# Vision tower on one core: the next image's first two heads scored in FF2, the head loop two heads ahead

## The chip, the cores and the metric

The kernel runs on one core of one Trainium2 chip. The metric is device time in microseconds of one execution. A core has TensorE (PE, with weight loads as PEld), VectorE (DVE), ScalarE (ACT), GpSimd (POOL) and SyncE (SP, here the issuer of nearly all DMAs), each with its own instruction queue that runs in order and waits on semaphores.

## The reference

Eight images of 256 x 256 go through a wavelet stage, get a class row (257 tokens, width 256), then four transformer layers with 16 heads of 64, and at last a mixture of experts. The part that the change touches is one layer for one image:

```python
q = q.reshape(b, s_len, H, DH); k = ...; val = ...
kr = (r @ W_r[i]).reshape(s_len, H, DH)
AC = jnp.einsum('bqhd,bkhd->bhqk', q + u, k)
BD = jnp.einsum('bqhd,khd->bhqk', q + v, kr)
prob = jax.nn.softmax((AC + BD) * inv_sqrt_d, axis=-1)
vec = jnp.einsum('bhqk,bkhd->bqhd', prob, val).reshape(b, s_len, H * DH)
h = layer_norm(h + vec @ W_o[i], ln1_g[i], ln1_b[i])
ff = jax.nn.relu(h @ W_ff1[i] + b_ff1[i]) @ W_ff2[i] + b_ff2[i]
h = layer_norm(ff, ln2_g[i], ln2_b[i])
```

## The kernel before

Matrices are kept as a high and a low float16 part, and a product is three matmuls (high x high, high x low, low x high: `TERMS`). Nearly every result that PE leaves in a PSUM bank is therefore copied twice: ACT writes the high half, DVE subtracts it from the bank for the low half (`p_part`, `o_part`, `v_part`, the FF1 copies). For queries and keys POOL makes both halves from a float32 copy in `rel`, a ring of four slots.

Each engine has one program, written out by hand: `body(at, l, b, kind)` for each of 32 steps (4 layers of 8 images), image after image. The order of its lines is the order of the queue; there is no planner. Semaphore counts run through (`at(32, n)` is the n-th of 32 signals of this step). Kinds: OPENING (the very first), ENTRY (first image of the layers 1 to 3), MIDDLE (18 of them), CLOSING (last image of the layers 0 to 2), TAIL (layer 3, six images, with expert routing beside it, `kind.routes`) and FINAL.

A step goes through these stages:

- **Class scores** (L1928): the class row of all heads, 24 small matmuls into bank 6; DVE takes the minimum (L2345), ACT the exponential (L2158).
- **Head loop**, h = 0 to 15. PE: scores of head h, four matmuls into the banks 0 and 1 (L1937, L1938), one slot of the next image's projections (`project`, six matmuls, L1844; in the closing step eight projections of positions besides), then `transposes(at, h - 1)` (L1893), four transposes of float32 exponentials into bank 2 or 3. DVE: row minimum of the negated scores with the position term `cb` added, two instructions per head (L2356), key copies (`take_k`, L2258) at odd h, and the low half of head h - 2's transposed exponentials (`p_part`, L2318). ACT: two exponentials per head with the row sum (L2162), query copies at even h (`take_q`, L2097), the high half of head h - 1's transposed exponentials (L2147), and at odd h the class column of two heads (L2187). POOL: both halves of each projection (L1730, L1732) and parts of the norm. The exponentials lie in `E`, a ring of EB = 4 heads.
- **After the loop**: PV products of two heads each (`pv`, L1905, 12 matmuls) for c = 0 and 1, the last head's transposes between them; transposes of the inverse sums and the class columns (L1999); `key` copies; then for c = 0 to 7 a spread of the inverse sums (L2014), the class part (L2018) and the further PV products, with copies on ACT and DVE.
- **W_o** (L2033), the first norm, the next image's values (`project_v`, L1860).
- **FF1**: eight chunks of six matmuls (L2064) into the banks `FB` = 2, 3, 6, 7. For even chunks ACT writes the high half from the bank (L2226), DVE a float32 copy into `rel[:, 0]` (L2474) and the low half from it (L2468). For odd chunks ACT writes float32 into `rel[:, 1]` (L2225) and the high half (L2226), DVE the low half (L2465). `rel[:, 0]` and `rel[:, 1]` are written again only when the previous pair's low half is made (`ff1_lo`).
- **FF2**: 48 matmuls into the banks 4 and 5 (L2076), in the order first output half, chunks 0 to 5; second, chunks 0 to 5; first, 6 and 7; second, 6 and 7. Then ACT's squares (L2236) and DVE's copies (L2504, L2292) for the second norm, whose rest runs inside the next head loop.

SP stacks the projected queries and keys of an image for its scores by DMA (`stack(at, part)`, L1538, 12 DMAs for each half of the heads), after POOL's last split of that half and when the previous image's scores of those heads are done. Before the change the whole loop waits for both halves:

```python
pe.wait_ge(stack_in, at(384, 384))
for h in range(H):
    for qt in range(QT):
        if h:
            pe.wait_ge(s_ok, at(32, 2 * h + qt - 1))
        q = qs[:, h, qt * P:(qt + 1) * P]
```

In the entry steps the class values go to DRAM and come back as `vbd` (`store_vcls`, `load_vbd`) once `class_v` (L1870) has run in the loop at h = 11. Before the first step a prologue projects the first image alone, and ACT loads the position term `cb` by DMA (L2131) between its class values and its first query copy.

## Time and profile before

| | us |
|---|---|
| median of 3 runs (lowest, highest) | 2553.95 (2551.61, 2559.08) |
| the profiled execution: its own time | 2552.9 |
| its span, first to last instruction | 2551.1 |
| PE busy / DVE / ACT / POOL in the span | 2229.0 / 1851.4 / 1599.2 / 1187.2 |
| steps of the image loop, from 174.9 us on | 32 |

The profile shows one execution. A line of the timeline is one instruction (or several merged, xN): start, busy time, engine, line of the kernel, operation, what is written from what, and in brackets the idle time of the engine just before it with what ended it. PE's matmuls are pipelined, so the time from start to start is what one costs the queue, and the busy time of PE is more than that; ACT's and DVE's instructions overlap a little in the same way.

### The profile page before, as it was taken

Reading aid. Unit: us, or ns where it says so; the run is one execution under the profiler, and the core shown is the slowest. Engines: PE = TensorE matmul, PEld = TensorE weight load, DVE = VectorE, ACT = ScalarE, POOL = GpSimd, SP = SyncE. Lnnn points to the kernel's source line nnn. Section 1 sums busy time; section 2 is a strip of 40 time slices with the busy share of each in tenths; the row PEclk is TensorE's granted clock in tenths of the full one; section 3 lists DMA queues with packets and bytes.
Section 4 is the critical chain, followed back from the end, with each engine's and each line's share of the span. In section 5 each row is a group of like instructions: output and inputs, shape, how many; then the busy total and the mean of one; then the engine's idle time right before and its main releaser. Section 6 shows DMA issues by size and latency. Waiting matters only on the chain.

```text
span 2551.1 us, 61172 instructions
## 1 busy us (share of the span) xinstructions
PE 2229.0 (87%) x19318; PEld 1654.4 (65%) x19318; DVE 1851.4 (73%) x5687; ACT 1599.2 (63%) x4853; POOL 1187.2 (47%) x2205
## 2 busy tenths in 40 slices
PE   0249999999989999999989999999899999987998
PEld 0127777777767777777766677777677777665665
DVE  8827777777777777777757777777678877776543
ACT  2216777777667777766656677776677766665322
POOL 3025555554455555554545555554565555541211
PEclk9679999999999999999999999999999999999999
DMA  4354444445554444444644444455533343355110
GB/s 165 83 149 100 123 105 104 110 106 149 148 147 122 108 106 107 108 121 139 183 124 116 111 106 108 102 149 147 151 102 92 98 102 94 98 148 183 51 47 22
DMA packets 378059, 295.35 MB, mean 116 GB/s; under 512 B 45087, under 2 KB 350721, under 8 KB 376739
## 3 DMA queue, kind: packets, MB, share of 16 engines
q1 hardware_dynamic: 370603, 272.41, 41.0%
q10 hardware_dynamic: 4864, 12.68, 1.4%
q0 software_dynamic: 2272, 6.35, 0.7%
q8 instruction: 158, 2.59, 0.4%
q14 instruction: 162, 1.33, 0.2%
HBM read 137.71 MB, written 72.07 MB: 82 GB/s over the span
## 4 chain that ended last, share of the span: by engine, by line
ACT 30%; PE 27%; DVE 15%; issue 7%; SPq 6%; POOL 5%; DMA 4%; DVEq 0%; ACTq 0%; POOLq 0%
ACT e_rows L2162 12%; ACT pt L2147 4%; SPq L1538 4%; PE bk L1279 4%; PE bk L2033 3%; PE bk L2076 3%; PE bk L1905 3%; ACT rel L2097 3%; DVE x L2419 3%; DVE o_rows L2327 3%; ACT pt L2226 2%; PE bk L1893 2%; PE bk L1844 2%; POOL arena L1732 2%; DVE pt L2465 1%
## 5 line engine op out<-in xcount | busy, mean ns | idle before, releaser
L2162 ACT ACTIVATE e_rows<-e_rows,nb 128x257 f32<-128x257 f32 x1024 | 516.8, 516 | 45.8 <-DVE nb L2356 45.1
L2356 DVE CUSTOM_DVE_ANT_0 e_rows<-bk,arena 128x257 f32<-128x257 f32 x1024 | 390.4, 418 | 77.1 <-PE bk L1938 75.8
L1844 PE MATMUL bk<-hin,arena 128*128 128x257 f16 x3072 | 423.5, 275 | 14.3 <-ACT rel L2097 6.9
L2318 DVE TENSOR_TENSOR pt<-bk,pt 128x512 f16<-128x512 f32 x512 | 353.9, 691 | 64.2 <-ACT pt L2147 51.7
L1893 PE MATMUL bk<-ident,e_rows 128*128 128x128 f32 x2048 | 324.1, 281 | 49.3 <-ACT e_rows L2162 28.3
L1732 POOL TENSOR_TENSOR arena<-rel,arena 128x257 f16<-128x257 f32 x496 | 327.3, 660 | 41.3
L1730 POOL TENSOR_SCALAR arena<-rel 128x257 f16<-128x257 f32 x496 | 202.8, 409 | 300.0 <-ACT rel L2097 295.7
L1844 PEld LDWEIGHTS bk<-hin,arena 128*128 128x128 f16 x3072 | 297.8, 98 | 65.1 <-issue 12.9
L2147 ACT ACTIVATE pt<-bk 128x512 f16<-128x512 f32 x512 | 310.1, 606 | 7.0 <-PE bk L1893 7.0
L1893 PEld LDWEIGHTS bk<-ident,e_rows 128*128 128x128 f32 x2048 | 221.6, 141 | 135.1 <-ACT e_rows L2162 113.3
L1937 PE MATMUL bk<-arena 128*128 128x257 f16 x1024 | 256.3, 275 | 12.2 <-DMA arena<-arena 11.7
L1780 POOL TENSOR_SCALAR wf<-wf 128x256 f32<-128x256 f32 x216 | 93.0, 430 | 370.7 <-DMA wf<-in_w_dram 189.7
L1938 PE MATMUL bk<-arena 128*128 128x257 f16 x1024 | 255.9, 275 | 0.0
L1905 PE MATMUL bk<-pt,arena 128*64 128x257 f16 x3072 | 222.1, 280 | 16.2 <-DVE x L2419 15.0
L2162 ACT ACTIVATION_READ_ACCUMULATOR e_rows<-e_rows,nb 128x1 f32 x1024 | 211.9, 207 | 0.0
L2076 PE MATMUL bk<-pt,w_rest 128*128 128x257 f16 x1536 | 181.0, 274 | 29.8 <-DVE pt L2465 29.8
L2033 PE MATMUL bk<-o_rows,w_rest 128*128 128x257 f16 x1536 | 191.1, 274 | 9.8 <-DVE o_rows L2327 8.1
L1905 PEld LDWEIGHTS bk<-pt,arena 128*64 128x64 f16 x3072 | 151.6, 110 | 70.6 <-DVE x L2419 44.6
L2064 PE MATMUL bk<-hres,w_rest 128*128 128x257 f16 x1536 | 178.6, 275 | 19.1 <-DVE hres L2452 18.3
L1788 POOL TENSOR_TENSOR wh<-wf,wh 128x256 f16<-128x256 f32 x264 | 182.5, 691 | 22.1
L2076 PEld LDWEIGHTS bk<-pt,w_rest 128*128 128x128 f16 x1536 | 147.2, 98 | 58.3 <-DVE pt L2465 38.4
L2064 PEld LDWEIGHTS bk<-hres,w_rest 128*128 128x128 f16 x1536 | 145.9, 98 | 57.8 <-DVE hres L2452 33.4
(329 smaller groups left out, 4197.1 us busy)
## 6 DMA issues: line engine op xcount, KB each, us to landing
arena<-arena SPq DMA_DIRECT2D x768, 128.5 KB
wf<-in_w_dram SPq DMA_DIRECT2D x168, 128.0 KB, 2.8
w_split_dram<-wh SPq DMA_DIRECT2D x168, 128.0 KB, 2.3
xs_dram<-in_c_blank_dram SPq DMA_DIRECT2D x24, 772.5 KB
wf<-in_we_dram SPq DMA_DIRECT2D x96, 128.0 KB, 2.7
we_split_dram<-wh SPq DMA_DIRECT2D x96, 128.0 KB, 1.9
w_rest<-w_split_dram SPq DMA_DIRECT2D x12, 1024.0 KB, 17.3
arena<-we_split_dram SPq DMA_DIRECT2D x8, 1536.0 KB, 12.7
```

The source lines that it names most:

```text
L1732: pool.tensor_tensor(dst[:, 1, j % NP, :], rel[:, s % RB_, :], dst[:, 0, j % NP, :], ALU.subtract).then_inc(proj_lo, 1)
L1844: r_ = mm(bank[4 + s % 2][:, 0:S], wcol(a, C_QKV, k, 3 * HD, chunk_at(s)), hin[:, m, k, :], start=i == 0, stop=i == 5)
L1893: r_ = pe.transpose(bank[2 + h % 2][:, (kt * QT + qt) * P:(kt * QT + qt + 1) * P], E[:, h % EB, qt, kt * P:(kt + 1) * P], ident[:, :])
L1905: mm(o[DH * s_:DH * (s_ + 1), 0:S], vs[:, a, kt, h * DH:(h + 1) * DH], pt[:, h, m, kt, :], start=kt + i == 0, stop=False)
L1937: mm(bank[qt][:, 0:S], q, kh[:, h, :], start=True, stop=False)
L2033: r_ = mm(bank[4 + m_][:, 0:S], wcol(a, C_O, c, D, m_), o2[:, m, c, :], start=False, stop=(c == NP - 1 and i == 2))
L2064: r_ = mm(bank[FB[j % 4]][:, 0:S], wcol(a, C_1, k, DF, j), hmid[:, m, k, :], start=i == 0, stop=i == 5)
L2076: r_ = mm(bank[4 + m_][:, 0:S], wcol(a, C_2, c, D, m_), hid[:, m, c, :], start=c + i == 0, stop=(c == FC - 1 and i == 2))
L2147: act.activation(pt[:, h, 0, :, 0:IMG], bank[2 + h % 2][:, :].rearrange("p (k s) -> p k s", k=QT), ACT.Copy).then_inc(p_hi, 1)
L2162: act.activation(E[:, h % EB, qt, :], E[:, h % EB, qt, :], ACT.Exp, bias=nb[:, 2 * h + qt:2 * h + qt + 1], scale=-1.0, accum_out=sums[:, q ...
L2318: v.tensor_tensor(pt[:, h, 1, :, 0:IMG], bank[2 + h % 2][:, :].rearrange("p (k s) -> p k s", k=QT), pt[:, h, 0, :, 0:IMG], ALU.subtract).t ...
L2356: v.tensor_tensor_reduce(E[:, h % EB, qt, :], bank[qt][:, 0:S], cb[:, h, :], -SCORE, 3e38, ALU.add, ALU.min, nb[:, 2 * h + qt:2 * h + qt + ...
```

## The change

Five edits, all in `attention_stage`:

1. `AHEAD = 2`: in the head loop PE makes scores of head h + 2, DVE the minima of h + 2, ACT the exponentials and class column of h + 2, while transposes and ACT's copy are those of head h itself and DVE's copy that of h - 1. There are 14 heads of scores, minima and exponentials left in the loop.
2. Heads 0 and 1 of the next image are made in FF2: PE puts head 0's scores before the last two chunks of the first output half, behind a new wait for the next image's values (`v_lo`), and head 1's after FF2. DVE makes head 0's minima behind its value copies and class queries, and head 1's behind the norm's copies. ACT makes head 0's exponentials behind its value copies and head 1's behind the squares. The prologue does the same for the first image.
3. FF1's float32 copies take four slots of `rel` in place of two; each waits for the low half two pairs back.
4. `stack_in` becomes two semaphores; PE waits for a half before head 0 or head 8.
5. Moves: `pv(0)` and `pv(1)` stand before the last two heads' transposes (not where `kind.routes`); DVE's last sums before its last but one copy; PE waits for the last query copy before the key transposes; in the prologue class values go before the wait for constants, and ACT's load of the position term after its third query copy.

```diff
-                                         src[rows, lo[half], c0:c0 + NP // 2, :]).then_inc(stack_in, 16)
+                                         src[rows, lo[half], c0:c0 + NP // 2, :]).then_inc(stack_in[part], 16)
...
+            def scores(at, h):
+                if h in (0, NP):
+                    pe.wait_ge(stack_in[h // NP], at(192, 192))
+                for qt in range(QT):
+                    if h:
+                        pe.wait_ge(s_ok, at(32, 2 * h + qt - 1))
+                    q = qs[:, h, qt * P:(qt + 1) * P]
+                    mm(bank[qt][:, 0:S], q, kh[:, h, :], start=True, stop=False)
+                    mm(bank[qt][:, 0:S], q, kl[:, h, :], start=False, stop=True).then_inc(s_done, 1)
...
-            pe.wait_ge(const_ok, CONST)
             first = At(pe, 0)
             class_v()
+            pe.wait_ge(const_ok, CONST)
...
+            pe.wait_ge(v_lo, 4)
+            for h in range(AHEAD):
+                scores(first, h)
...
-                pe.wait_ge(stack_in, at(384, 384))
                 for h in range(H):
-                    for qt in range(QT):
...
+                    if h + AHEAD < H:
+                        scores(at, h + AHEAD)
...
-                    if h:
-                        transposes(at, h - 1)
+                    if h == H - 2 and not kind.routes:
+                        values_free(at, atl, b, kind)
+                        pv(at, 0)
+                    if h == H - 1 and not kind.routes:
+                        pe.wait_ge(s_ok, at(32, 32))
+                        pv(at, 1)
+                    transposes(at, h)
...
-                pv(at, 0)
-                transposes(at, H - 1)
-                pe.wait_ge(s_ok, at(32, 32))
-                pv(at, 1)
-
+                if kind.routes:
+                    values_free(at, atl, b, kind)
+                    pv(at, 0)
+                    pe.wait_ge(s_ok, at(32, 32))
+                    pv(at, 1)
+
+                if kind.next:
+                    pe.wait_ge(q_ok, at1(8, 8))
...
                 for m_, cs in ((0, range(FC - 2)), (1, range(FC - 2)), (0, range(FC - 2, FC)), (1, range(FC - 2, FC))):
+                    if kind.next and m_ == 0 and cs.stop == FC:
+                        pe.wait_ge(v_lo, at1(4, 4))
+                        scores(at1, 0)
...
+                if kind.next:
+                    scores(at1, 1)
...
-            load_position_term(first)
             for s in range(0, 2 * NP, 2):
                 take_q(first, s)
+                if s == 4:
+                    load_position_term(first)
...
+                    if h + AHEAD < H:
+                        exponentials(at, h + AHEAD)
...
-                        act.wait_ge(ff1_lo, at(8, j - 1))
-                        act.activation(rel[:, 1, :], bank[FB[j % 4]][:, 0:S], ACT.Relu, bias=par[:, BF1 + j:BF1 + j + 1], scale=1.0 / WS).then_inc(relu_ok, 1)
+                        act.wait_ge(ff1_lo, at(8, max(j - 3, 0)))
+                        act.activation(rel[:, 1 + j // 2 % 2 * 2, :], bank[FB[j % 4]][:, 0:S], ACT.Relu, bias=par[:, BF1 + j:BF1 + j + 1], scale=1.0 / WS).then_inc(relu_ok, 1)
...
+                    exponentials(at1, 0)
...
+                if kind.next:
+                    exponentials(at1, 1)
...
-                    if h >= EB:
-                        v.wait_ge(t_done, at(16, h - EB + 1))
-                        v.wait_ge(ecol_ok, at(8, (h - EB) // 2 + 1))
...
+                    if h + AHEAD < H:
+                        if h + AHEAD >= EB:
+                            v.wait_ge(t_done, at(16, h + AHEAD - EB + 1))
+                            v.wait_ge(ecol_ok, at(8, (h + AHEAD - EB) // 2 + 1))
+                        maxima(at, h + AHEAD)
...
-                    if h >= 2:
-                        p_part(at, h - 2)
+                    if h == H - 1:
+                        last_sums(at)
+                    if h:
+                        p_part(at, h - 1)
...
-                    v.wait_ge(ff1_lo, at(8, max(j - 1, 0)))
-                    v.tensor_scalar(rel[:, 0, :], bank[FB[j % 4]][:, 0:S], par[:, BF1W + j:BF1W + j + 1], 0.0, ALU.add, ALU.max).then_inc(rel_ok, 1)
+                    v.wait_ge(ff1_lo, at(8, max(j - 3, 0)))
+                    v.tensor_scalar(rel[:, j // 2 % 2 * 2, :], bank[FB[j % 4]][:, 0:S], par[:, BF1W + j:BF1W + j + 1], 0.0, ALU.add, ALU.max).then_inc(rel_ok, 1)
...
+                    v.wait_ge(t_done, at(16, 16))
+                    v.wait_ge(ecol_ok, at(8, 8))
+                    if kind.closing:
+                        v.wait_ge(cb_in, 16 * (l + 2))
+                    maxima(at1, 0)
...
+                if kind.next:
+                    maxima(at1, 1)
```

## Rows read from the trace of the kernel before

**Rows 1.** Windows: stretch, its length, busy us (xcount) of PE, PEld, DVE, ACT, POOL.

```profile
core 0: us, PE busy (x) PEld busy (x) DVE busy (x) ACT busy (x) POOL busy (x), PEclk, DMA share, GB/s
1056.00:1084.00 28.00, 27.05 (x232) 22.02 (x230) 24.46 (x93) 27.80 (x99) 21.20 (x40) 1.00 0.35 87
1108.40:1120.30 11.90, 10.88 (x96) 9.17 (x96) 7.92 (x20) 6.39 (x15) 2.95 (x6) 1.00 0.44 121
```

**Rows 2.** Timeline of ACT, two heads of the loop in the middle image.

```profile
1065.74 0.52 ACT L2162 ACTIVATE e_rows<-e_rows,nb 128x257 f32<-128x257 f32 x1
...
1066.72 0.60 ACT L2147 ACTIVATE pt<-bk 128x512 f16<-128x512 f32 x1
...
1067.30 0.52 ACT L2162 ACTIVATE e_rows<-e_rows,nb 128x257 f32<-128x257 f32 x1
...
1069.12 0.53 ACT L2162 ACTIVATE e_rows<-e_rows,nb 128x257 f32<-128x257 f32 x1
```

**Rows 3.** Timeline of ACT: class exponential, head 2's, the next image's class exponential.

```profile
1056.17 0.51 ACT L2158 ACTIVATE ec<-ec,nbc 128x257 f32<-128x257 f32 x1 [1.23 <-DVE nbc L2345]
...
1060.40 0.50 ACT L2162 ACTIVATE e_rows<-e_rows,nb 128x257 f32<-128x257 f32 x1
...
1122.14 0.51 ACT L2158 ACTIVATE ec<-ec,nbc 128x257 f32<-128x257 f32 x1 [1.23 <-DVE nbc L2345]
```

**Rows 4.** Timeline of PE at the loop's end: last transposes, first reciprocal spread.

```profile
1084.48 0.66 PE L1893 MATMUL bk<-ident,e_rows 128*128 128x128 f32 x4 [0.35 <-ACT e_rows L2162]
...
1087.29 0.28 PE L2014 MATMUL bk<-pkr,sel 128*128 128x257 f16 x1
```

**Rows 5.** Timeline of PE: FF1, FF2 in two parts, class scores, head 0's scores.

```profile
1108.41 5.49 PE L2064 MATMUL bk<-hres,w_rest 128*128 128x257 f16 x48 [0.69 <-DVE hres L2452]
...
1113.74 1.82 PE L2076 MATMUL bk<-pt,w_rest 128*128 128x257 f16 x15
...
1116.57 3.83 PE L2076 MATMUL bk<-pt,w_rest 128*128 128x257 f16 x33 [1.01 <-DVE pt L2465]
...
1120.33 0.85 PE L1928 MATMUL bk<-arena,qbd 128*32 128x257 f16 x24
...
1121.11 0.28 PE L1937 MATMUL bk<-arena 128*128 128x257 f16 x1
```

**Rows 6.** Timeline of DVE and POOL in FF1 and FF2 of the same image.

```profile
1113.75 0.42 DVE L2465 TENSOR_TENSOR pt<-rel,pt 128x257 f16<-128x257 f32 x1
...
1115.56 0.67 POOL L1788 TENSOR_TENSOR wh<-wf,wh 128x256 f16<-128x256 f32 x1
1115.91 0.61 DVE L2465 TENSOR_TENSOR pt<-rel,pt 128x257 f16<-128x257 f32 x1
...
1117.97 1.29 DVE L2264 TENSOR_TENSOR arena<-bk,arena 128x512 f16<-128x512 f32 x2
...
1121.68 0.42 DVE L2345 CUSTOM_DVE_ANT_0 ec<-bk,cc 128x257 f32<-128x257 f32 x1
...
1122.03 0.42 DVE L2356 CUSTOM_DVE_ANT_0 e_rows<-bk,arena 128x257 f32<-128x257 f32 x1
```

**Rows 7.** Timeline of the opening; the last row is the DMA issue of `cb`.

```profile
152.69 0.48 ACT L2097 ACTIVATE rel<-bk,u 128x257 f32<-128x257 f32 x1 [5.67 <-DMA cc_dram<-cc]
...
161.73 10.20 SPq L1538 DMA_DIRECT2D arena<-arena  x12
...
174.40 8.85 SPq L1538 DMA_DIRECT2D arena<-arena  x12
...
185.97 0.40 PE L1937 MATMUL bk<-arena 128*128 128x257 f16 x1 [11.68 <-DMA arena<-arena]
...
arena<-cc_dram ACTq DMA_DIRECT2D x1, 2056.0 KB, 13.6
```

**Rows 8.** PE's waits in the entry step from 1257 to 1334 us: total, times, longest.

```profile
PE bk L2018 <- DMA vbd<-vbd_dram: 4.9, 1, 4.9
PE bk L1870 <- POOL hcls L1761: 1.9, 1, 1.9
```

**Rows 9.** Windows, as in group 1: the head loop of a tail step.

```profile
2078.70:2108.00 29.30, 27.17 (x243) 21.91 (x241) 27.36 (x115) 27.94 (x98) 20.94 (x40) 1.00 0.26 57
```

More of the change, by code:

```diff
@@ L1916, in _, with values_free @@
                 project_v(first, u)
+            pe.wait_ge(v_lo, 4)
+            for h in range(AHEAD):
+                scores(first, h)
+            def values_free(at, atl, b, kind):
+                pe.wait_ge(pc_lo, at(1, 1))
+                if kind.routes and b >= 2:
+                    pe.wait_ge(r.slot_ok, b - 1)
+                if kind.ln2:
+                    pe.wait_ge(vy_ok, at(1, 0))
+                if kind.closing:
+                    pe.wait_ge(cc_ok, atl(1, 1))
+                if kind.entry:
+                    pe.wait_ge(vcls_lo, atl(2, 2))
             def body(at, l, b, kind):
@@ L2147, in p_part, with exponentials, class_column @@
                 act.activation(pt[:, h, 0, :, 0:IMG], bank[2 + h % 2][:, :].rearrange("p (k s) -> p k s", k=QT), ACT.Copy).then_inc(p_hi, 1)
+            def exponentials(at, h):
+                for qt in range(QT):
+                    act.wait_ge(s_ok, at(32, 2 * h + qt + 1))
+                    act.activation(E[:, h % EB, qt, :], E[:, h % EB, qt, :], ACT.Exp, bias=nb[:, 2 * h + qt:2 * h + qt + 1],
+                                   scale=-1.0, accum_out=sums[:, qt, h:h + 1]).then_inc(e_ok, 1)
+            def class_column(at, h):
+                act.wait_ge(e_ok, at(32, 2 * h + 2))
+                both = E[:, (h - 1) % EB:(h - 1) % EB + 2, :, CLS].rearrange("p b k -> p k b").unsqueeze(2).broadcast_to([P, QT, 3, 2])
+                first, i = class_row(h - h % 4, 0), (h - 1) % 4
+                act.activation(ecol[:, :, first:first + 12].rearrange("p k (c i) -> p k c i", i=4)[:, :, :, i:i + 2], both, ACT.Copy).then_inc(ecol_ok, 1)
+            for h in range(AHEAD):
+                exponentials(first, h)
             def o_part(at, c):
@@ L2159, in body @@
                 for h in range(H):
-                    for qt in range(QT):
-                        act.wait_ge(s_ok, at(32, 2 * h + qt + 1))
-                        act.activation(E[:, h % EB, qt, :], E[:, h % EB, qt, :], ACT.Exp, bias=nb[:, 2 * h + qt:2 * h + qt + 1],
-                                       scale=-1.0, accum_out=sums[:, qt, h:h + 1]).then_inc(e_ok, 1)
+                    if h + AHEAD < H:
+                        exponentials(at, h + AHEAD)
                     for s in slots(h, kind):
@@ L2181, in body @@
                         spread_position_term(atl)
-                    if h % 2:
-                        act.wait_ge(e_ok, at(32, 2 * h + 2))
-                        both = E[:, (h - 1) % EB:(h - 1) % EB + 2, :, CLS].rearrange("p b k -> p k b").unsqueeze(2).broadcast_to([P, QT, 3, 2])
-                        first, i = class_row(h - h % 4, 0), (h - 1) % 4
-                        act.activation(ecol[:, :, first:first + 12].rearrange("p k (c i) -> p k c i", i=4)[:, :, :, i:i + 2], both, ACT.Copy).then_inc(ecol_ok, 1)
-                p_part(at, H - 1)
+                    if h == 0:
+                        class_column(at, 1)
+                    if h % 2 and h + AHEAD < H:
+                        class_column(at, h + AHEAD)
                 if kind.closing:
@@ L2323, in inverse_sums, with last_sums, maxima @@
                 v.reciprocal(out, sums[:, :, 4 * j:4 * j + 4].unsqueeze(2).broadcast_to([P, QT, 2, 4])).then_inc(rs_ok, 1)
+            def last_sums(at):
+                v.wait_ge(e_ok, at(32, 32))
+                inverse_sums(3)
+                v.wait_ge(ec_ok, at(1, 1))
+                v.tensor_copy(ecr[:, 0, :], ec[:, CLS:S]).then_inc(rs_ok, 1)
+                v.reciprocal(ecr[:, 1, :], sumc[:, :]).then_inc(rs_ok, 1)
+            def maxima(at, h):
+                for qt in range(QT):
+                    v.wait_ge(s_done, at(32, 2 * h + qt + 1))
+                    v.tensor_tensor_reduce(E[:, h % EB, qt, :], bank[qt][:, 0:S], cb[:, h, :], -SCORE, 3e38,
+                                           ALU.add, ALU.min, nb[:, 2 * h + qt:2 * h + qt + 1]).then_inc(s_ok, 1)
+            v.wait_ge(cb_in, 16)
+            for h in range(AHEAD):
+                maxima(first, h)
             def o_part(at, c):
```

44 lines of the change are left out of this document (9 added, 35 removed).

## The prediction

> **What bounds the kernel now.** I read the windows first, then each engine's timeline through one middle image (1056 to 1122 us), then the opening and the odd images. In the head loop [rows 1] ACT is busy 27.80 of 28.00 us and PE 27.05; PE's granted clock is 1.00, its upper level, 2.4 GHz. PE's figure flatters it, as its records overlap; ACT's is a queue with no holes. ACT's own starts show it [rows 2]: two exponentials .98 us, one transposed-score copy with a class column .58, two exponentials and the query copy and the other copy 1.82: 3.38 us for two heads, with nothing waited for. PE needs for the same two heads 8 score, 12 projection and 8 transpose instructions; FF1's 48 matmuls take 5.33 us [rows 5], .111 each, so 3.1 us. **The loop is ACT's, and PE stands 8% behind it.** The image takes 65.97 us, and 4.23 us pass from its class exponential to head 2's exponentials [rows 3]. Outside the loop PE sets the pace, with a hole of 1.01 us in FF2, where it waits for DVE's low halves of FF1 [rows 5]. The first image stands alone: PE waits 11.68 us for the stacked halves [rows 7].
>
> **The change, part by part** (times of the image at 1122, those of the loop before carried on by 65.97).
>
> FF1's copies. Before, each pair of chunks waits until the previous pair's low half has left its only slot. With four slots ACT and DVE follow PE: PE makes two chunks in 1.33 us, DVE needs three operations of some .4 us and ACT three of .37. The sixth low half is then ready at about 114.7, before PE wants it (1113.74 + 15 x .111 = 1115.4), and the 1.01 us hole goes.
>
> Scores in FF2. PE does 36 of the 48 FF2 matmuls (to 117.74), head 0's four score matmuls (.44), the last 12 (to 119.5), head 1's scores (to 119.96) and the class scores, which took .78 [rows 5]: 120.74. It was 1121.11 before. The added wait for V: behind it stand 12 FF2 matmuls, and behind those the squares of the second norm. FF1's last chunk is copied 1.6 us after 113.74 (an estimate, two ACT and one DVE copy of .42 and handovers), V's two halves take 1.29 [rows 6]: 116.7, 1 us before PE asks. Free, with that cover.
>
> Then DVE is late. Before, it was free 1.35 us after FF2 ended (1120.33 to 1121.68) [rows 5, 6]. Now FF2 ends at 119.5, and the squares on ACT stand behind two exponentials, some .3 late: DVE is free at 121.15, and only then makes head 1's maxima, .35 each by start to start [rows 6]. PE gets its bank for head 2 at 121.6 and has stood .9 us: this is the wait that takes the place of the old hole. ACT does head 1's exponentials from 121.6, the class exponential (.5) from 122.6 and head 2's from 123.1. Before, head 2's began at 126.37 [rows 3], but of the 4.23 us before them .50 + 1.96 were class and heads 0 and 1; the other 1.77 (query copy, transposed copy, class column, two norm operations) is still owed. 123.1 + 1.77 = 124.9: **1.5 us earlier**, and ACT goes on without holes, since scores two heads ahead give its inputs more time.
>
> The end of the loop. From the last transposes to the first reciprocal spread passed 2.81 us [rows 4], two PV products and four key transposes within. Now both products stand before the last transposes, where ACT has two heads without exponentials and PE catches up: two projections (1.33), two PV products and two transposes there take PE longer than the 1.3 us of copies that ACT still has, some .3 us; against that goes the time that PE stood before its last transposes (.35) [rows 4]. I count nothing; bounds .7 worse, .5 better. The added wait for the last query copy is free: that copy is on ACT two transposed copies earlier. SP's 24 stacking DMAs per image stay in number and order, and their holds on scores are met earlier; those halves were wanted at the loop's start and are now wanted in FF2, some 3 us earlier, with the whole W_o stage between. POOL gets nothing new and keeps idle time (21.20 busy of 28.00 in the loop) [rows 1].
>
> So a middle image gains 1.5. **18 of them: 27 us.** Bounds: .5 (the V wait and DVE each take half a microsecond) and 2.2 (no stall at head 2).
>
> The three closing images have 24 projections in the loop instead of 16 and are PE's, which loses 8 score matmuls and its end waits: 1.5 each, 4.5 (bounds 2 to 6). The three entry images wait twice for something else [rows 8]: 1.9 us for the class rows from POOL, then 4.9 for the class values' way through DRAM. That chain hangs on query copies, which now stand behind two more exponentials, .9 later at equal heads: I take .5 us lost each, -1.5 (+1 to -6). The six tail images have routing on DVE, busy 27.36 of 29.30 us [rows 9]; they lose 1.4 us of maxima from the loop but keep their PV products after it: 1.0 each, 6 (0 to 10). The last image: 1.0.
>
> The opening. The query copy stood 5.67 us behind ACT's wait for the position term [rows 7]; this wait moves two copies on and the whole first projection about 6 us up, class values' matmuls starting before the constants. The first half's DMAs start at about 155.8 instead of 161.73, are issued in 10.2 us and have landed 2.7 us after (185.97 less 174.40 + 8.85): 168.7. The position term's own transfer (13.6 us from 152.3) runs against them: +2, say 171. Scores start there instead of at 185.97: **15 us**. The second half lands at about 182, when head 8's scores are due (171 + 6 x 1.7 + 2). Bounds: 6 (both transfers slow each other, the half lands at 180) and 17.
>
> **Sum:** 27 + 4.5 - 1.5 + 6 + 1 + 15 = 52 us. The profiled execution takes 2552.9 (span 2551.1 and 1.8 around it), so 2500.9; the median of the runs is 1.05 above it: **2502 us**.
>
> **A rule weighed.** Beside POOL's chunk subtraction, one of DVE's low-half subtractions takes .61 us instead of .42 [rows 6]. That is one of nine in this stretch; in the sum it is nothing, since V has 1 us to spare. The Trainium skill, SBUF — State Buffer, Who interferes with whom, says that a DVE instruction with two SBUF inputs and a GpSimd instruction that reads SBUF block each other for a whole instruction. The trace agrees with the direction by that pair; no row shows a whole POOL operation of delay on each.
>
> **The rivals.** *The copies collide with POOL (chance .13).* Crowded into 6 us instead of 8, more of them meet POOL: with .19 more on each of nine, 1.7 us, .7 more than the cover; 27 images lose .7, 19 us: 2521. For it: the pair above. Against: POOL is busy 2.95 us of FF's 11.90 [rows 1]. *The opening gains little (.08):* the first half lands at 180: 2511. For it: cb's 13.6 us. Against: it is issued earlier than the stack. *More than I count (.14):* DVE finishes the norm sooner and PE never stands before head 2; 2.2 for each middle and closing image, 15 more: 2487. *DVE's queue decides (.05), slower than before:* the next image's maxima stand in one queue with V's split, class queries and the norm. If they come more than 2.2 us later than I have them (1.5 + 15 / 21), ACT starves at the start of every loop; with 3 us late, each middle and closing image loses 1.5 instead of gaining and the others 1: 2554 + 31 + 9 - 15 = 2579. For it: DVE is already the last before the loop, 1.35 us after FF2. Against: in FF it is busy 7.92 us of 11.90 [rows 1]. *The change does not take effect (.02):* if transposes, not exponentials, limited ACT, two heads ahead would be an empty reordering; with FF1 and the opening in vain too: 2550.
>
> **How the numbers follow.** My forecast (gain 40 to 65) .58, the rivals as given. The range must leave out 2 in 10: it takes the forecast with its bounds, the opening and most of the collision: 2484 to 2527. A measurement of this kernel tells .3%, 7.7 us, from no change. Faster: .58 + .13 + .08 + .14 = .93, less .03 for what I don't see; same .02 + .03 = .05; slower .05.
>
> **What would show it.** In the changed trace: FF2 without the 1.01 us hole; no wait for V before head 0's scores; a stand of PE before head 2's scores near .9 us, released by DVE's maxima; middle images 64.5 us apart (64.2 to 65.4); head loop still ACT's at 3.38 a pair; entry images within 1 us of before; scores of the first image near 171. Wrong if middle images stay above 65.5, if ACT's pair of heads shows holes behind DVE, or if the opening gives under 6 us.

## The result and the profile after

The changed kernel takes 2541.4 us (median of 5 runs, 2538.3 to 2542.4) against 2555.6 of the kernel before in the same set (2551.6 to 2559.1): ratio 0.9941, 95% interval 0.9927 to 0.9956. It is faster by 14 us where I had forecast 52, and lies outside my range. The profiled execution has a span of 2539.6 us, 11.5 under that of before.

Where the spans differ, step by step, from one class exponential to the next (the first record of its line in each step of ACT's timeline; before, after, forecast of the change):

| stretch | before | after | difference | forecast |
|---|---|---|---|---|
| start to the second image's class exponential | 251.8 | 241.4 | -10.4 | -15 |
| 18 middle images | 1187.2 | 1183.6 | -3.6 | -27 |
| 3 closing images | 209.3 | 210.1 | +0.8 | -4.5 |
| 3 entry images | 227.4 | 232.6 | +5.2 | +1.5 |
| 6 tail images | 407.9 | 405.0 | -2.9 | -6 |
| the last image and what follows | 267.6 | 266.9 | -0.7 | -1 |

Of the 40 us missing here, 23 are in the middle images and 5 in the closing ones. The timeline of PE through FF of one of them and, below "...", the end of its loop:

```profile
1030.94 5.49 PE L2084 MATMUL bk<-hres,w_rest 128*128 128x257 f16 x48 [0.53 <-DVE hres L2498]
1036.27 4.15 PE L2099 MATMUL bk<-pt,w_rest 128*128 128x257 f16 x36
1040.26 0.27 PE L1896 MATMUL bk<-arena 128*128 128x257 f16 x1
...
1040.69 1.49 PE L2099 MATMUL bk<-pt,w_rest 128*128 128x257 f16 x12
1042.02 0.28 PE L1896 MATMUL bk<-arena 128*128 128x257 f16 x1
...
1042.56 0.85 PE L1954 MATMUL bk<-arena,qbd 128*32 128x257 f16 x24
1044.45 0.28 PE L1896 MATMUL bk<-arena 128*128 128x257 f16 x1 [1.04 <-DVE nb L2374]
...
1068.94 0.60 PE L1905 MATMUL bk<-ident,e_rows 128*128 128x128 f32 x4
1069.46 0.84 PE L1846 MATMUL bk<-hin,arena 128*128 128x257 f16 x6
1070.23 0.86 PE L1917 MATMUL bk<-pt,arena 128*64 128x257 f16 x12
1071.02 0.65 PE L1905 MATMUL bk<-ident,e_rows 128*128 128x128 f32 x4
1071.51 0.83 PE L1846 MATMUL bk<-hin,arena 128*128 128x257 f16 x6
1072.27 0.86 PE L1917 MATMUL bk<-pt,arena 128*64 128x257 f16 x12
1073.06 0.66 PE L1905 MATMUL bk<-ident,e_rows 128*128 128x128 f32 x4
1073.55 0.38 PE L2019 MATMUL bk<-ident,rs 128*128 128x128 f32 x2
...
1075.65 0.28 PE L2034 MATMUL bk<-pkr,sel 128*128 128x257 f16 x1 [0.72 <-DVE pkr L2455]
```

The hole of 1.01 us in FF2 [rows 5] is gone, the scores (L1896) stand where they should, and PE waits 1.04 us before head 2's. The last transposes (L1905, 1073.06) come behind two projections (L1846) and two PV products (L1917) made since 1069.46. What DVE does while PE waits before head 2: both norm copies and the sum stand ahead of head 1's maxima (L2374).

```profile
1042.84 0.48 DVE L2555 TENSOR_SCALAR x<-bk,par 128x257 f32<-128x257 f32 x1 [0.73 <-ACT sq L2273]
1043.25 0.42 DVE L2331 TENSOR_TENSOR t<-sq 128x257 f32<-128x257 f32 x1
1043.58 0.48 DVE L2555 TENSOR_SCALAR x<-bk,par 128x257 f32<-128x257 f32 x1
1043.98 0.41 DVE L2374 CUSTOM_DVE_ANT_0 e_rows<-bk,arena 128x257 f32<-128x257 f32 x1
```

ACT's timeline of the same image: head 1's exponentials, the class exponential, head 2's, the last exponential, and the copies of the transposed scores of heads 14 and 15:

```profile
1044.43 0.51 ACT L2178 ACTIVATE e_rows<-e_rows,nb 128x257 f32<-128x257 f32 x1 [1.33 <-DVE nb L2374]
...
1045.43 0.49 ACT L2199 ACTIVATE ec<-ec,nbc 128x257 f32<-128x257 f32 x1
...
1045.92 0.49 ACT L2178 ACTIVATE e_rows<-e_rows,nb 128x257 f32<-128x257 f32 x1
...
1070.23 0.55 ACT L2178 ACTIVATE e_rows<-e_rows,nb 128x257 f32<-128x257 f32 x1
...
1071.71 0.60 ACT L2173 ACTIVATE pt<-bk 128x512 f16<-128x512 f32 x1
1073.75 0.60 ACT L2173 ACTIVATE pt<-bk 128x512 f16<-128x512 f32 x1 [1.44 <-PE bk L1905]
```

The same last exponential and last copy in the kernel before:

```profile
1083.81 0.53 ACT L2162 ACTIVATE e_rows<-e_rows,nb 128x257 f32<-128x257 f32 x1
...
1085.17 0.60 ACT L2147 ACTIVATE pt<-bk 128x512 f16<-128x512 f32 x1 [0.16 <-PE bk L1893]
```

The larger half of the case is in two brackets: before, ACT waits .16 us for its last copy; after, 1.44. An image split at five such records shows where time moves, since A and B below repeat within .02 us from one middle image to the next (C scatters by up to 1 us, E by .5). **The stage table** has the means over 12 middle images (the third to sixth of each layer); A: class exponential to the last exponential (to the start of its last record, which reads the row sum, .40 us behind its own start); B: from there to the first reciprocal spread; C: to FF1; D: FF1; E: FF2's start to the next class exponential.

| kernel | A | B | C | D | E | image |
|---|---|---|---|---|---|---|
| before | 28.04 | 3.08 | 21.01 | 5.35 | 8.38 | 65.86 |
| changed | 25.20 | 5.03 | 21.01 | 5.32 | 9.20 | 65.76 |
| slots alone | 28.04 | 3.09 | 21.02 | 5.32 | 7.22 | 64.69 |
| slots and opening | 28.07 | 3.09 | 21.08 | 5.32 | 7.23 | 64.79 |
| changed, slots undone | 25.18 | 5.03 | 21.12 | 5.34 | 10.73 | 67.40 |
| changed, maxima first | 25.21 | 5.03 | 21.13 | 5.32 | 8.46 | 65.16 |
| + head 1's scores early | 25.19 | 5.04 | 21.14 | 5.32 | 8.19 | 64.88 |
| + PV behind keys | 25.20 | 4.57 | 21.08 | 5.33 | 8.46 | 64.64 |
| + both | 25.21 | 4.58 | 21.03 | 5.32 | 8.19 | 64.34 |
| + both, reciprocals first | 25.20 | 4.17 | 21.01 | 5.33 | 8.19 | 63.89 |
| one head ahead | 26.71 | 3.65 | 21.04 | 5.33 | 8.20 | 64.94 |

The change takes 2.84 us out of the loop (A), puts 1.95 behind the last exponential (B) and .82 ahead of the class exponential (E): .10 us an image is left. Not all of A's 2.84 was saved. Two heads' exponentials are 1.96 of it; the other .88 is a query copy and a transposed copy that now stand behind the last exponential, and so count in B. B's 1.95 are these .88 and 1.28 more of waiting for the last copy (1.44 for .16), less .22 by which the way from the last transposes to the first spread got shorter (1075.65 - 1073.06 = 2.59 for 2.81).

The opening, first SP's timeline (the two halves of the stack), then PE's:

```profile
154.73 15.31 SPq L1540 DMA_DIRECT2D arena<-arena  x12
...
172.40 9.15 SPq L1540 DMA_DIRECT2D arena<-arena  x12
```

```profile
173.32 0.37 PE L1896 MATMUL bk<-arena 128*128 128x257 f16 x1 [8.45 <-DMA arena<-arena]
```

The first half is issued 7 us sooner than in [rows 7] but takes 15.31 us instead of 10.20; scores start at 173.3 instead of 186.0, where I had 171.

### The profile page after: what moved, and what is told of

Same layout as the page of the kernel before. It is cut to its first block, busy times and chain, and to the rows that moved or that the text cites. A ratio compares the mean times of both kernels' runs of the same rounds, so it can differ in the third digit from the quotient of the medians.

```text
span 2539.6 us, 60248 instructions
## 1 busy us (share of the span) xinstructions
PE 2217.2 (87%) x19318; PEld 1661.2 (65%) x19318; DVE 1844.1 (73%) x5687; ACT 1592.7 (63%) x4853; POOL 1191.3 (47%) x2205
## 3 DMA queue, kind: packets, MB, share of 16 engines
q8 instruction: 158, 2.59, 0.4%
## 4 chain that ended last, share of the span: by engine, by line
PE 40%; ACT 19%; DVE 17%; POOL 7%; issue 5%; SPq 4%; DMA 3%; DVEq 0%; ACTq 0%; POOLq 0%
ACT e_rows L2178 8%; PE bk L2084 6%; PE bk L2099 4%; PE bk L2053 4%; PE bk L1917 4%; PE bk L1279 4%; PE bk L1846 4%; PE bk L1905 4%; DVE x L2465 3%; ACT pt L2173 3%; DVE o_rows L2383 2%; SPq L1540 2%; POOL arena L1734 2%; DVE pt L2357 2%; POOL arena L1732 2%
## 5 line engine op out<-in xcount | busy, mean ns | idle before, releaser
L2374 DVE CUSTOM_DVE_ANT_0 e_rows<-bk,arena 128x257 f32<-128x257 f32 x1024 | 391.5, 420 | 83.7 <-PE bk L1897 82.9
L1846 PE MATMUL bk<-hin,arena 128*128 128x257 f16 x3072 | 421.5, 274 | 5.5 <-ACT rel L2122 3.6
L1905 PE MATMUL bk<-ident,e_rows 128*128 128x128 f32 x2048 | 317.0, 277 | 44.9 <-DVE pt L2357 34.3
L1846 PEld LDWEIGHTS bk<-hin,arena 128*128 128x128 f16 x3072 | 294.4, 97 | 55.1 <-ACT rel L2122 9.9
L1905 PEld LDWEIGHTS bk<-ident,e_rows 128*128 128x128 f32 x2048 | 228.2, 141 | 115.9 <-ACT e_rows L2178 90.7
L1896 PE MATMUL bk<-arena 128*128 128x257 f16 x1024 | 259.8, 276 | 39.7 <-DVE nb L2374 31.3
L1897 PE MATMUL bk<-arena 128*128 128x257 f16 x1024 | 258.7, 275 | 0.0
L1917 PE MATMUL bk<-pt,arena 128*64 128x257 f16 x3072 | 224.3, 283 | 22.7 <-DVE x L2465 17.9
L1917 PEld LDWEIGHTS bk<-pt,arena 128*64 128x64 f16 x3072 | 153.9, 111 | 80.1 <-DVE x L2465 47.8
L2237 ACT ACTIVATE sq<-bk 128x257 f32<-128x257 f32 x256 | 97.8, 385 | 132.0 <-PE bk L2034 129.6
```

Source lines behind the costliest of these rows:

```text
L1846: r_ = mm(bank[4 + s % 2][:, 0:S], wcol(a, C_QKV, k, 3 * HD, chunk_at(s)), hin[:, m, k, :], start=i == 0, stop=i == 5)
L1896: mm(bank[qt][:, 0:S], q, kh[:, h, :], start=True, stop=False)
L1905: r_ = pe.transpose(bank[2 + h % 2][:, (kt * QT + qt) * P:(kt * QT + qt + 1) * P], E[:, h % EB, qt, kt * P:(kt + 1) * P], ident[:, :])
L1917: mm(o[DH * s_:DH * (s_ + 1), 0:S], vs[:, a, kt, h * DH:(h + 1) * DH], pt[:, h, m, kt, :], start=kt + i == 0, stop=False)
L2374: v.tensor_tensor_reduce(E[:, h % EB, qt, :], bank[qt][:, 0:S], cb[:, h, :], -SCORE, 3e38, ALU.add, ALU.min, nb[:, 2 * h + qt:2 * h + qt + ...
```

## The experiments

The kernel before was run again beside each group of kernels, with medians from 2550.9 to 2555.6 us, so a difference of times between kernels of different groups is good to some 4 us. Where less than that matters, the stage table decides.

**Two parts alone, and two orders.** The slots and the opening were put by themselves into the kernel before.

FF1's slots alone ("..." stands for lines or arguments left out, here and below; the low halves read the same slots):

```
-    act.wait_ge(ff1_lo, at(8, j - 1))
-    act.activation(rel[:, 1, :], ...)
+    act.wait_ge(ff1_lo, at(8, max(j - 3, 0)))
+    act.activation(rel[:, 1 + j // 2 % 2 * 2, :], ...)
...
-    v.wait_ge(ff1_lo, at(8, max(j - 1, 0)))
-    v.tensor_scalar(rel[:, 0, :], ...)
+    v.wait_ge(ff1_lo, at(8, max(j - 3, 0)))
+    v.tensor_scalar(rel[:, j // 2 % 2 * 2, :], ...)
```

> The kernel before with nothing changed but FF1's four slots. Theory P (PE's queue is what an image takes; a gain is a wait taken from PE and not given back): the 1.0 us hole in FF2 goes from 31 steps and nothing takes its place: 28 us faster than before, more than the whole change gave (12). Theory A (ACT's queue decides in the head loop): the loop starts 1.0 us earlier too, about the same 28 us. Theory S (the hole only moves to the next wait on PE): under 8 us.

Measured: 2523.0 us, ratio 0.9882 (0.9855 to 0.9909), 31 us under before, so more than the whole change brings. PE's timeline has FF2 in one piece:

```profile
1037.14 5.48 PE L2076 MATMUL bk<-pt,w_rest 128*128 128x257 f16 x48
1042.55 0.85 PE L1928 MATMUL bk<-arena,qbd 128*32 128x257 f16 x24
```

E falls by 1.16 and nothing else moves in a middle image. The theory of a hole that only moves on is out; the other two asked for the same 28 us, and this run does not part them.

The opening alone:

```
-            pe.wait_ge(const_ok, CONST)
             first = At(pe, 0)
             class_v()
+            pe.wait_ge(const_ok, CONST)
...
-            load_position_term(first)
             for s in range(0, 2 * NP, 2):
                 take_q(first, s)
+                if s == 4:
+                    load_position_term(first)
...
-                pe.wait_ge(stack_in, at(384, 384))
                 for h in range(H):
+                    if h in (0, NP):
+                        pe.wait_ge(stack_in[h // NP], at(192, 192))
```

> The kernel before with the opening's edits alone: class values ahead of the wait for constants, the position term's load after the third query copy, a wait for each stacked half. All theories: the opening gives what it gave in the whole change, 10 to 13 us, once; middle images as before, 65.9 us. If it gives 12 alone, the rest of the change is worth nothing.

Measured: 2542.3 us, ratio 0.9957 (0.9946 to 0.9968): 11.4 us. The two parts together would be 42 us; the whole change gives 14. So the third part, the two heads made ahead (with the moves that go with them), costs about 28 us.

The PV products as before the change:

```
-                    if h == H - 2 and not kind.routes:
+                    if h == H - 1 and not kind.routes:
                         values_free(at, atl, b, kind)
                         pv(at, 0)
-                    if h == H - 1 and not kind.routes:
-                        pe.wait_ge(s_ok, at(32, 32))
-                        pv(at, 1)
                     transposes(at, h)
...
-                    pe.wait_ge(s_ok, at(32, 32))
-                    pv(at, 1)
+                pe.wait_ge(s_ok, at(32, 32))
+                pv(at, 1)
```

> The changed kernel with the first two PV products where they stood before: the first ahead of the last transposes, the second behind them. Theory P with the end of the loop as the place: PE's 0.8 us of PV leaves the way to the last transposes and fills its 0.7 us wait before the first spread: 0.7 to 1.0 us for each of 21 middle and closing images, 15 to 20 us faster than the changed kernel. Theory A as I predicted it (the order at the end counts nothing): within 4 us of the changed kernel.

Measured: 2536.9 us, ratio 0.9940 (0.9918 to 0.9962). B in a middle image is 4.96 instead of 5.03: both products still stand ahead of the key transposes, and a shift between them is worth nothing. ACT's wait for its last copy did fall, to 1.17 us in the image at 1044.6, but the key transposes came .61 us later; so a shorter wait on ACT is worth nothing here unless PE's work up to the key transposes gets shorter too. The 15 to 20 us that theory P wanted are not there. What it gives is in the closing (B 6.18 for 6.80) and entry images (4.32 for 6.02).

Head 1's maxima ahead of the norm's copies:

```
+                if kind.next:
+                    maxima(at1, 1)
                 v.wait_ge(z1_lo, at(2, 2))
                 for m in range(KC):
...
-                if kind.next:
-                    maxima(at1, 1)
```

> The changed kernel with DVE's minima of the next image's head 1 ahead of the second norm's three operations instead of behind them. Theory P: PE's 1.04 us wait before head 2's scores goes, but the norm's copies are now 0.7 us later and the next image's first projection waits for them: net 0.4 us for each of some 27 images, 11 us faster than the changed kernel. Theory A: ACT has head 1's exponentials 1.1 us earlier and keeps it: 25 to 30 us faster.

Measured: 2516.2 us, ratio 0.9855 (0.9834 to 0.9877), 25 us under the changed kernel. The timeline of PE, the first of head 2's scores and the next projection:

```profile
1037.92 0.28 PE L1896 MATMUL bk<-arena 128*128 128x257 f16 x1
...
1039.03 0.82 PE L1846 MATMUL bk<-hin,arena 128*128 128x257 f16 x6 [0.50 <-issue]
```

The wait of 1.04 is gone, .50 of another comes behind it (by the code, the projection writes the bank that the norm's copy reads), E falls by .74. A and B do not move, and the image loses .60 of it (C is .12 longer). This is near theory A's 25 to 30 us (ACT has head 1's exponentials earlier and keeps it) and far from theory P's 11, which took PE's new wait from the gain.

**The price of the heads ahead.** Slots and opening together in the kernel before:

> The kernel before with FF1's four slots and the whole opening (position term's wait behind two query copies, class values ahead of the constants, halves waited for apart), and nothing made ahead. Additive theory: the two parts touch nothing of each other, 30.8 of the slots and 11.4 of the opening: 2511 to 2513, ratio .983 to .984, middle images 64.8 apart. Rival, overlap (the opening's gain is partly lost when the loop no longer has slack): 2517 or more. If it is the additive one, the heads made ahead cost the changed kernel some 29 us against this one.

Measured: 2509.8 us, ratio 0.9832 (0.9816 to 0.9849). The parts add up to within 2 us, and the heads ahead cost 28 to 32 us (28 by the gains of 41.7 and 14.2 against the kernel before beside each, 31.6 by 2541.4 - 2509.8): in a middle image A -2.87, B +1.94, E +1.97.

The changed kernel with FF1's copies in two slots again (the first diff, backwards):

> The changed kernel with FF1's copies back in two slots (opening and heads ahead kept). If the slots are worth the same 31 us with the heads made ahead as without: 2541 + 31 = 2572 (2568 to 2576), middle images 66.9, so that heads ahead with the opening are 30 us worse than the opening alone. Rival (the stall in FF2 and the stall before head 2 cover each other, so that the slots gain little here): 2541 to 2555.

Measured: 2588.6 us, ratio 1.0149 (1.0132 to 1.0166). In this kernel the slots are worth 47 us (51 by the two gains), not 31, so both readings missed. PE's timeline of FF2 (second part), head 0's scores and head 2's:

```profile
1060.19 2.50 PE L2099 MATMUL bk<-pt,w_rest 128*128 128x257 f16 x21 [0.96 <-DVE pt L2511]
1062.93 0.28 PE L1896 MATMUL bk<-arena 128*128 128x257 f16 x1 [0.24 <-DVE arena L2303]
...
1067.14 0.28 PE L1896 MATMUL bk<-arena 128*128 128x257 f16 x1 [1.05 <-DVE nb L2374]
```

The late low halves open the hole of .96 and also push V's split behind PE's wait for it (.24), while the stall before head 2 stays: three waits for DVE one behind the other. With the slots the cover that I counted on for V holds: no wait stands at 1040.26 above.

**What B and E are made of.** The second PV product behind the key transposes (on top of the maxima ahead):

```
-                    if h == H - 1 and not kind.routes:
-                        pe.wait_ge(s_ok, at(32, 32))
-                        pv(at, 1)
...
                     r_.then_inc(key_done, 1)
+                pe.wait_ge(s_ok, at(32, 32))
+                pv(at, 1)
                 for c in range(NP):
```

> The changed kernel with head 1's maxima ahead of the norm's copies, and now the second PV product behind the key transposes instead of ahead of the last scores' transposes. Theory E (the end of the loop, from the last exponential to the first reciprocal spread, is a chain of PE, ACT and DVE in which the second PV product and the last projection stand in front of the last transposes): the last transposes come .8 earlier, the PV product fills PE's .7 wait before the spread: .6 to .8 less per image, 27 images, 2516 - 19 = 2497 (2494 to 2501); middle images 64.4 to 64.6. Theory Q (ACT's queue through the loop decides, the end hides behind it): 2514 to 2517, middle images 65.1 still.

Measured: 2510.8 us, ratio 0.9835 (0.9818 to 0.9851). The 12 middle images of the table are at 64.64, just above my 64.4 to 64.6, but only 5.4 us of the 19 are there: 6.3 in all 18 middle images and 1.3 in the closing, and the tails gave 3.7 back (C 21.5 instead of 20.9). That loss goes with TensorE's clock: in two of the six tails C is 23.1 and 22.9 us at a mean granted clock of .93 (one such tail, of 22.3 us, without this edit), in the others 20.2 to 21.2 at 1.00. B fell by .46, not .7, because the key transposes then waited .33 us for DVE's last reciprocals.

Head 1's scores ahead of the last six FF2 matmuls:

```
+                    if kind.next and m_ == 1 and cs.stop == FC:
+                        scores(at1, 1)
                     for c in cs:
...
-                if kind.next:
-                    scores(at1, 1)
```

> The changed kernel with head 1's maxima ahead of the norm's copies, and head 1's scores ahead of the last six FF2 matmuls of the second half instead of behind them. Theory E: PE then waits for head 0's second maxima there (.2 to .3), the squares come .5 later, and the time before head 2 changes by less than .3 per image: 2510 to 2518. Theory Q (ACT waits for its first exponentials, so earlier is better): head 1's exponentials .5 earlier, 2503. Slower than 2520 would say that the second norm's chain counts.

Measured: 2511.2 us, ratio 0.9842 (0.9825 to 0.9858), E 8.46 to 8.19, as theory E had it.

Then the sums. All four orders together; the fourth is this one:

```
+                    if h == H - 1:
+                        last_sums(at)
                     for s in slots(h, kind):
                         if s % 2:
                             take_k(at1, s)
...
-                    if h == H - 1:
-                        last_sums(at)
```

> The changed kernel with four orders mended together: head 1's maxima ahead of the norm's copies, head 1's scores ahead of the last six FF2 matmuls, the second PV product behind the key transposes, and DVE's last reciprocals ahead of the last key copy. Theory E (what two heads ahead save in the loop, 2.84 us an image, is given back in the stretch from the last exponential to the first reciprocal spread and in the stretch from FF2 to the class exponential, and these four orders shorten those two): .28 from the scores and .46 from the PV product add up, the reciprocals give .15 to .3 more: middle images 64.1 to 64.3, 2490 to 2500, below the kernel with slots and opening alone (2510). Theory Q (the stages share one total, what is saved at one end is waited for at the other): 2506 to 2511.

Measured: 2494.5 us, ratio 0.9768 (0.9755 to 0.9782), as theory E had it; middle images at 63.89, just under its 64.1. B is 4.17, E 8.19. PE's timeline of the end of the loop:

```profile
1054.47 0.63 PE L1905 MATMUL bk<-ident,e_rows 128*128 128x128 f32 x4
1054.93 0.38 PE L2014 MATMUL bk<-ident,rs 128*128 128x128 f32 x2
...
1055.46 1.52 PE L1917 MATMUL bk<-pt,arena 128*64 128x257 f16 x24
1057.04 0.28 PE L2031 MATMUL bk<-pkr,sel 128*128 128x257 f16 x1
```

The key transposes follow the last transposes at once, and two PV products (x24) fill the time that PE had stood before the spread (.72 above).

The same without the fourth order:

> The same without the change to DVE's last reciprocals. Theory E: the shortenings seen alone (5.0 us for the scores, 5.4 for the PV product) add up: 2516.2 - 10.4 = 2506 (2502 to 2508). Theory Q: 2511, no better than either alone.

Measured: 2500.3 us, ratio 0.9801 (0.9787 to 0.9814), just under the 2502 to 2508 of theory E, 6 us better than the sum of its parts in time; in a middle image the parts add to .02 (65.16 - .28 - .52 = 64.36 against 64.34). The reciprocals' place is worth .45 an image in the stage table (.41 of it B).

One head ahead instead of two (AHEAD = 1, no scores, maxima or exponentials of head 1 in FF2, PV products as before the change):

> The changed kernel with one head ahead instead of two: only head 0's scores, maxima and exponentials are made in FF2, the PV products stand where they stood before the change, slots and opening kept. Theory E (the second head is the one that DVE's and PE's queues make dear: behind the norm at one end, two PV products and a projection in front of the last transposes at the other): the loop saves half of 2.84, the stretch behind the last exponential grows by little (3.1 to 3.6 instead of 5.0), the stretch from FF2 to the class exponential grows by .45 over the slots alone (7.2 to 7.7): middle images 64.0 to 64.5, 2490 to 2504. Rival (any head ahead costs as much at the ends as it saves, in proportion): half of two heads' loss of 31.6, 2525.

Measured: 2521.0 us, ratio 0.9877 (0.9862 to 0.9892). A loses 1.36 and B gains .56, as theory E had it, but E is 8.20, not 7.7: .97 more than with no head ahead, of which head 0's scores on PE are .44; the squares and the norm's copies behind head 0's exponentials are the likely rest, not priced apart. The middle images are .15 slower than without any head ahead, and the tails 7 us in all; two of the tails have C at 23.9 and 23.8 us at a granted clock of .93, some 3 us above the same two of the kernel without heads ahead, at 1.00. The rival's 2525 is nearer than my 2504.

In the tails, DVE's low halves of the last three heads ahead of that step's routing:

```
+                    early = kind.routes and h >= H - 3
+                    if early:
+                        if h == H - 1:
+                            last_sums(at)
+                        p_part(at, h - 1)
...
-                    if h:
+                    if h and not early:
                         p_part(at, h - 1)
```

> The kernel with all four orders mended, and in the six tail images DVE's low halves of the transposed scores of the last three heads (and the last reciprocals) ahead of the routing operations of that step instead of behind them. Theory E (the stretch behind the last exponential is a chain of handovers, and in the tails, 6.57 us against 4.17 in a middle image, DVE's routing stands in it: PE waits 1.29 us there for a low half): 1 to 1.5 us less in each of six tails, 2494.5 - 7 = 2487 (2485 to 2490). Rival (DVE's queue is full in the tails, and the routing that is moved back delays the next thing by as much): 2493 to 2496, and the stretch to FF1 longer by what the end got shorter.

Measured: 2501.6 us, ratio 0.9799 (0.9785 to 0.9812), 7 us slower than without it: the rival, and more. PE's timeline in a tail without it:

```profile
2052.42 0.63 PE L1905 MATMUL bk<-ident,e_rows 128*128 128x128 f32 x4 [1.29 <-DVE pt L2354]
...
2058.90 0.86 PE L1917 MATMUL bk<-pt,arena 128*64 128x257 f16 x12 [0.70 <-DVE x L2462]
```

and with it:

```profile
2057.91 0.63 PE L1905 MATMUL bk<-ident,e_rows 128*128 128x128 f32 x4 [0.46 <-DVE pt L2354]
2059.21 0.85 PE L1917 MATMUL bk<-pt,arena 128*64 128x257 f16 x12 [0.68 <-issue]
...
2065.00 0.86 PE L1917 MATMUL bk<-pt,arena 128*64 128x257 f16 x12 [1.90 <-DVE x L2467]
...
2066.32 1.50 PE L1917 MATMUL bk<-pt,arena 128*64 128x257 f16 x12
```

DVE's last routing copy, in the same tail:

```profile
2058.95 0.16 DVE L360 CAST route_slot<-route_slot_f 128x2 int32<-128x2 f32 x1
```

The wait for the low half shrinks, but PE then stands .68 before its first PV product. By the code it waits there for `slot_ok`, which DVE's copy L360 gives: that copy, at 2053.58 and ahead of the first PV product without this edit, is now among the last of DVE's queue and ends .1 us before PE goes on. So B stays at 6.56. PE then stands 1.90 us among the further PV products (.70 before), and C grows by 2.0 on average in four of the six tails. Behind the stand TensorE's clock is low: 12 products take 1.50 us instead of .86, and the granted clock is .64 from 2065 to 2068 us and .84 to 2072, where it is 1.00 in the same stretch of the kernel without this edit. All four longer tails have it (.92 to .93 over C), the two others do not. Why the stand itself grew stays open: the trace names DVE and, behind it, an ACT copy that waits 2.87 us for a PE result long finished.

## Why the prediction was wrong

**The step that failed is "The end of the loop ... I count nothing; bounds .7 worse, .5 better".** In the prediction's terms it is 1.06 us worse in every middle image: ACT waits 1.28 us more for its last copy, and .22 comes back behind it. (Stage B grows by 1.95, but .88 of that is work which has only crossed its border.) I let PE's work ahead of the last transposes (two projections, two PV products, two transposes) exceed ACT's remaining copies by "some .3 us", and the prediction shows no working for that figure. In the changed trace these six pieces take 4.09 us of PE's queue (1069.46 to 1073.55). Between ACT's copies of heads 14 and 15 PE made a projection, a PV product and the transposes, and ACT stood 1.44 us. This is the mis-sized number: 1.44 for .3.

Up to that point the sum was close. I had ACT's queue 1.5 us earlier. Before, the last copy began 1085.17 - 1056.17 + 8.38 = 37.38 us after FF2's start, .16 of it a wait; after, 1073.75 - 1036.27 = 37.48, 1.44 of it a wait. So ACT was ready for it 1.2 us sooner (.3 of my 1.5 had gone before head 2's exponentials, see below), and 1.06 of that went at the end: .1 us an image is what the table shows. The reason lies one level up, in **"The loop is ACT's, and PE stands 8% behind it"**. This is true of the loop and of nothing else, and 8% was generous: I counted the transposes at a score matmul's .111 us each, but four of them take .49 (1071.02 to 1071.51), so that PE needs 3.2 of ACT's 3.38 us for two heads and stands 5% behind. Two heads ahead take eight score matmuls out of the loop, but PE keeps all its projections and PV products, and they gather at the end, where ACT has no exponentials left to hide them. I saw this crowd and did not lay out the queue of each engine there record by record.

The whole 1.5 us is of two things that should have been told apart: 1.16 from the slots, which the experiment with them alone shows as real, and the rest from the heads ahead, which turned out at +1.07 instead of -.3.

**The start of the loop.** FF1's copies and PE's FF2 went as written; PE's stand before head 2 was forecast at .9 and is 1.04; head 2's exponentials 9.36 us after FF2's start, measured 9.65: here are the .3. The step that I passed over is that this stand was taken as the order of nature. Moving head 1's maxima ahead of the norm's copies gave 25 us in the whole kernel. My rival "more than I count" named this wait, but as something that might go by itself, at 15 us.

**Closing images** (forecast -4.5, measured +.8): B grows from 3.33 to 6.80 there, as 24 projections meet the same crowd. **Entry images** (+1.5, measured +5.2): A falls 2.84, B grows 2.96 and E .92; the chain through DRAM did not get longer, as the waits in the entry step from 1236 to 1325 us show:

```profile
PE bk L2038 <- DMA vbd<-vbd_dram: 3.3, 1, 3.3
...
PE bk L1872 <- POOL hcls L1763: 2.2, 1, 2.2
```

[rows 8] had 4.9 and 1.9 for the same two. The rest is C, .69 us longer on average, and it goes with the clock: in the three entry images before, C is 22.2, 26.9 and 25.4 us at mean granted clocks of 1.00, .87 and .93; after, 26.5, 25.7 and 24.3 at .87, .87 and .86. PE's long stands for the class rows and for DRAM lie in or just ahead of this stage. How much of its length is the stands and how much the clock wasn't parted. **Tails** (-6, measured -2.9): B 3.60 to 6.39 took back most of A's 4.27. **The opening** (-15, measured -10.4; -11.4 alone): right in kind; the stack's first half took 15.31 us to issue instead of 10.2. That it lost to the 2056 KB transfer beside it is likely but wasn't isolated. Of the 12.7 us by which scores start sooner, the class scores take 1.4 us back (175.52 to 176.93): before, they were made in PE's wait for the stack, now they stand behind the first two heads' scores.

**The rivals.** "The copies collide with POOL" did not come: in the changed kernel's FF two of eight low halves take .63 us, both while POOL scales and rounds a weight chunk, and PE waits for neither, nor for V. Over the whole run 47 of the 256 low halves take over .55 us, against 45 in the kernel before, and the median stays at .42: the copies do not meet POOL more often. But the prediction read too little out of its one pair. In 70 of the 76 places of the changed trace where a POOL operation with over .15 us to go runs when such a low half starts, the low half ends .27 to .29 us after POOL's has ended: at 1037.12 it takes .63 us beside a POOL operation that ends at 1037.48, at 1166.00 it takes .89 beside one from 1165.88 to 1166.60. In the other six it is POOL's operation that gets longer (.70 to .96 us). So the one that comes second is held until the first is done, as the rule weighed in the prediction has it (the Trainium skill, SBUF — State Buffer, Who interferes with whom), and a copy can lose .47 us by it, not only .19. "DVE's queue decides" needed maxima 2.2 us late; they were .3 late. No rival of mine held that the heads ahead cost more than they save. That case ended at 2541, 14 us above my range, and it still came out faster only because slots and opening give 42 us; the heads ahead, the main part of the change, cost 28 or more. So the chance of .9 for faster came true, but not for the reason given: 27 us of the sum were to come from the middle images, which gave 3.6.

The kernel with all four orders mended takes 2494.5 us: 56 less than the kernel before in its set and 47 less than the changed one. In it the heads ahead are worth 15 us against slots and opening alone (2509.8). The remaining cost is B at 4.17 against 3.09 and E at 8.19 against 7.23.

## What to carry to other kernels

Work moved ahead of a saturated loop was paid for here at both of its ends: the loop's engine gained, and the work of the others crowded where its cover ran out. Price the stretch behind the last long operation by laying out each engine's queue there, not by busy shares. Where a change has independent parts, split the forecast by part, and look at which of two operations in one queue stands first: here the order of two DVE maxima and three norm operations was worth 25 us.

## What the runs showed that I had not expected

- Shortenings at either end of the loop add: .28, .52 and .45 us an image, in sum 65.16 to 63.89 against 63.91 by addition.
- A, the stretch of ACT's full queue, did not move by more than .03 us in any kernel with two heads ahead, whatever was done at its ends.
- The same four slots are worth 31 us in one order of work and 47 in another.
- SP issued the same 12 stacking DMAs in 10.20 us in the kernel before, in 15.31 and 9.15 in the changed one, so the time to issue is not a constant of the instruction.
- A stand of 1.9 us of PE in a tail was followed by some 3.5 us at half speed (granted clock .64 and .84 in the windows behind it), so that such a stand cost more than its own length; the scatter of C from run to run in tails and entry images goes with the granted clock.
